# Graph layers with segment means and an edge softmax on one core: softmax weights in the bank of the logits, and the first mean pass scanning from PSUM

## The reference, cut to what matters

```python
# one SAGE layer; relu behind the first two
msg = x[src]
mean = segment_sum(msg, dst) / maximum(count(dst), 1)
h = mean @ Wl.T + bl + x @ Wr.T
# after three layers
x = layernorm(x + h)

# attention over the edges of each source node
q = (x @ Wq)[src];  k = (x @ Wk)[dst];  ek = edges @ Wek
v = (x @ Wv)[dst];  ev = edges @ Wev
attn = einsum('ehd,ehd->eh', q, (k + ek) * scale) @ W_exp
ex = exp(attn - segment_max(attn, src)[src])
attn = ex / segment_sum(ex, src)[src]
agg = segment_sum(attn * (v + ev), src)
out = ((x @ Wv) - agg) @ W_out
x = layernorm(x + out)
```

## Time and profile before

| What | us |
|---|---|
| median of three runs | 2773.49 |
| the runs | 2766.67 to 2774.2 |
| the profiled execution, its own time | 2783.83 |
| its span, first to last instruction | 2782.0 |
| POOL busy in the span | 1855.1 (67%) |
| PE busy in the span | 1887.0 (68%) |
| DVE busy in the span | 1732.6 (62%) |
| ACT busy in the span | 1098.7 (39%) |

### The profile page before, as it was taken

The page is one execution under the profiler, slowest core; times in us unless marked ns, Lnnn a source line. Parts: engine busy times, 40 slices in busy tenths (PEclk is TensorE's granted clock), DMA queues, the critical chain, the costliest instruction groups (busy, mean ns, idle before and its releaser), DMA issues.

```text
span 2782.0 us, 43790 instructions
## 1 busy us (share of the span) xinstructions
PE 1887.0 (68%) x10441; PEld 1352.4 (49%) x10441; DVE 1732.6 (62%) x5671; ACT 1098.7 (39%) x2508; POOL 1855.1 (67%) x1895
## 2 busy tenths in 40 slices
PE   3546666999979999677777745777777777770000
PEld 1425655666656666455555533555555555550000
DVE  7757777677757777565555533777777787780000
ACT  7951110444434444122222213666666666660000
POOL 0046776776647665377777777777777777745776
PEclk7657899999989999788888877999999999995555
DMA  0014654988869997544444513444444444433231
GB/s 18 1 50 126 148 142 115 184 198 187 188 139 172 192 203 165 146 126 130 123 136 136 155 42 100 133 136 134 136 139 134 138 136 140 133 110 106 85 96 54
DMA packets 366724, 356.94 MB, mean 128 GB/s; under 512 B 46534, under 2 KB 288724, under 8 KB 366584
## 3 DMA queue, kind: packets, MB, share of 16 engines
q1 hardware_dynamic: 310136, 246.40, 29.3%
q0 software_dynamic: 56448, 109.10, 20.6%
HBM read 232.83 MB, written 129.11 MB: 130 GB/s over the span
## 4 chain that ended last, share of the span: by engine, by line
POOL 36%; PE 28%; issue 18%; DVE 10%; DMA 5%; ACT 1%; SPq 1%; POOLq 1%; DVEq 0%; ACTq 0%
POOL hsrc L659 15%; POOL GX L659 14%; PE bank L836 7%; POOL out_dram L713 4%; PE bank L856 4%; PE bank L758 3%; PE bank L879 3%; PE bank L871 3%; PE bank L869 3%; DMA GX<-in_x_dram,idx_a 2%; POOL x_prime L713 2%; DVE hsrc L1200 2%; PE bank L840 2%; DVE hsrc L1201 1%; PE bank L854 1%
## 5 line engine op out<-in xcount | busy, mean ns | idle before, releaser
L659 POOL DMA_INDIRECT GX<-mean_product,idx_a x392 | 412.5, 1052 | 128.2 <-issue 114.4
L659 POOL DMA_INDIRECT GX<-in_x_dram,idx_a x392 | 406.2, 1036 | 118.3 <-issue 111.2
L1025 ACT ACTIVATE logv<-mv,eps 128x4 f32<-128x4 f32 x294 | 87.0, 296 | 586.6 <-DVE mv L1331 586.5
L836 PE MATMUL bank<-h,wt 128*128 128x512 f32 x588 | 316.1, 648 | 0.0
L1359 DVE TENSOR_TENSOR_SCAN seg<-flag,seg,hsrc 128x512 f32<-128x512 bf16 x147 | 189.2, 1287 | 147.4 <-ACT hsrc L1037 82.0
L713 POOL DMA_INDIRECT x_prime<-normed,idx_b x196 | 199.5, 1018 | 98.1 <-issue 92.1
L659 POOL DMA_INDIRECT hsrc<-x_prime,idx_d x196 | 216.5, 1105 | 59.8 <-issue 59.8
L758 PE MATMUL bank<-ident,GX 128*128 128x128 f32 x588 | 108.5, 315 | 214.1 <-DMA GX<-in_x_dram,idx_a 174.2
L659 POOL DMA_INDIRECT hsrc<-x_prime,idx_c x196 | 210.1, 1072 | 59.8 <-issue 59.8
L758 PE MATMUL bank<-ident,hsrc 128*128 128x128 f32 x468 | 92.4, 332 | 216.6 <-DMA hsrc<-x_prime,idx_d 123.2
L713 POOL DMA_INDIRECT out_dram<-XN,idx_b x196 | 192.5, 982 | 61.5 <-issue 53.3
(11 more groups left out here) (226 smaller groups left out, 4702.8 us busy)
## 6 DMA issues: line engine op xcount, KB each, us to landing
mean_product<-prod SPq DMA_DIRECT2D x147, 256.0 KB, 3.9
hsrc<-mean_product SPq DMA_DIRECT2D x147, 256.0 KB, 4.2
XN<-in_x_dram SPq DMA_DIRECT2D x98, 256.0 KB, 6.3
x_prime<-normed SPq DMA_DIRECT2D x98, 256.0 KB, 3.9
XN<-x_prime SPq DMA_DIRECT2D x98, 256.0 KB, 4.5
out_dram<-normed SPq DMA_DIRECT2D x98, 256.0 KB, 2.1
flag<-same_dst_row SPq DMA_DIRECT2D x147, 128.0 KB
XN<-low_row SPq DMA_DIRECT2D x98, 128.0 KB, 3.7
```

What stands on the lines that cost most here:

```text
L659: pool.indirect_dma_start(buf[:, c.slot(U), t, :], None, table, bass.IndirectOffsetOnAxis(ap=idx[:, c.slot(U), t:t + 1], axis=0)).then_inc ...
L836: last = pe.matmul(psum[:, :], wt[:, T_R[i], :], before[:, c.slot(2), :], start=True, stop=not dst_phase)
L1025: act.activation(logv[:, s, :], mv[:, s, :, 1], ACT.Ln, bias=eps[:, 0:1]).then_inc(n_log.of(c), 1)
```

## The change

1. `weight` is no longer a piece of SBUF but bank 5 itself. DVE writes logit - maximum back into bank 5, ACT takes the exponential of bank 5 in place, the den scan, the product with v and the num scan read it there, and the product writes it there. dmax keeps one half, for decay.
2. The logit matmul of a chunk, which overwrites bank 5, waits for the num scan of the chunk before (a_num) instead of its dmax.
3. In mean0 PE turns into bank 5 and bank 2 by turns. DVE scans from that bank and waits for the turn; ACT copies the bank to hsrc after the scan and waits for the scan. PE's turn waits for the scan and the copy of two chunks before, instead of the copy of one before.
4. The second pair of look-up banks of mean0 is 6 and 7 instead of 2 and 6, and one matmul of table_sums writes the upper half of bank 0 instead of bank 2.

mean1, mean2, dst and rest keep their code. On each engine the instructions stand in the same order as before; what differs is their operands and waits.

```diff
-        dmax = part([2, CH])
+        dmax = part([CH])
         decay = part([CH])
-        weight = part([CH])
+        weight = bank[5]
...
+        def turn_bank(c):
+            return (5, 2)[c.slot(2)]
...
             def mean_turn(c):
                 pe.wait_ge(gathered.of(c), gathered.after(c))
-                pe.wait_ge(m_h.of(c), m_h.after(c, 1))
-                psum = bank[5]
+                if c.phase == "mean0":
+                    pe.wait_ge(m_h.of(c), m_h.after(c, 2))
+                    pe.wait_ge(m_seg.of(c), m_seg.after(c, 2))
+                    psum = bank[turn_bank(c)]
+                else:
+                    pe.wait_ge(m_h.of(c), m_h.after(c, 1))
+                    psum = bank[5]
...
-                pe.matmul(bank[2][:, 0:COLS + 1], last_row[:, :], marks_sum[:, 1, :], start=True, stop=True).then_inc(marks_turned, 1)
+                pe.matmul(bank[0][:, WIDE:WIDE + COLS + 1], last_row[:, :], marks_sum[:, 1, :], start=True, stop=True).then_inc(marks_turned, 1)
...
-                return ((0, 1), (2, 6))[c.slot(2)] if c.phase == "mean0" else (3, 4)
+                return ((0, 1), (6, 7))[c.slot(2)] if c.phase == "mean0" else (3, 4)
...
             def att_logit(c):
                 pe.wait_ge(a_qk.of(c), a_qk.after(c))
-                pe.wait_ge(a_dmax.of(c), a_dmax.free(c))
+                pe.wait_ge(a_num.of(c), a_num.after(c, 1))
...
             def mean_keep(c):
-                act.wait_ge(m_turned.of(c), m_turned.after(c))
                 i = int(c.phase[-1])
+                if i == 0:
+                    act.wait_ge(m_seg.of(c), m_seg.after(c))
+                else:
+                    act.wait_ge(m_turned.of(c), m_turned.after(c))
                 h = take_cols(hsrc, c.index() * CH, CH)
                 if i == 0:
-                    act.activation(h, bank[5][:, :], ACT.Copy).then_inc(m_h.of(c), 1)
+                    act.activation(h, bank[turn_bank(c)][:, :], ACT.Copy).then_inc(m_h.of(c), 1)
...
-                act.activation(decay[:, :], dmax[:, 0, :], ACT.Exp)
-                act.activation(weight[:, :], dmax[:, 1, :], ACT.Exp).then_inc(a_exp.of(c), 1)
+                act.activation(decay[:, :], dmax[:, :], ACT.Exp)
+                act.activation(weight[:, :], weight[:, :], ACT.Exp).then_inc(a_exp.of(c), 1)
...
             def mean_seg(c):
-                dve.wait_ge(m_h.of(c), m_h.after(c))
+                if c.phase == "mean0":
+                    dve.wait_ge(m_turned.of(c), m_turned.after(c))
+                    rows = bank[turn_bank(c)][:, :]
+                else:
+                    dve.wait_ge(m_h.of(c), m_h.after(c))
+                    rows = take_cols(hsrc, c.index() * CH, CH)
...
-                dve.tensor_tensor_scan(seg[:, c.slot(2), :], flag[:, c.slot(4), :], take_cols(hsrc, c.index() * CH, CH),
+                dve.tensor_tensor_scan(seg[:, c.slot(2), :], flag[:, c.slot(4), :], rows,
...
-                dve.tensor_tensor(dmax[:, 0, :], prev, reset, ALU.add).then_inc(a_step1.of(c), 1)
-                dve.tensor_tensor(dmax[:, 1, :], logit, top, ALU.subtract)
+                dve.tensor_tensor(dmax[:, :], prev, reset, ALU.add).then_inc(a_step1.of(c), 1)
+                dve.tensor_tensor(weight[:, :], logit, top, ALU.subtract)
                 dve.wait_ge(a_step1.of(c), a_step1.after(c))
-                dve.tensor_tensor(dmax[:, 0, :], dmax[:, 0, :], top, ALU.subtract).then_inc(a_dmax.of(c), 1)
+                dve.tensor_tensor(dmax[:, :], dmax[:, :], top, ALU.subtract).then_inc(a_dmax.of(c), 1)
```

More of the change, by code:

```diff
@@ L1376, in make_table @@
                 dve.wait_ge(marks_turned, 1)
-                link(dve.tensor_copy(marks_r[:, :], bank[2][:, 0:COLS + 1]))
+                link(dve.tensor_copy(marks_r[:, :], bank[0][:, WIDE:WIDE + COLS + 1]))
                 for a in range(2):
@@ L1407, in look_take @@
                 s = c.slot(2)
-                banks, width, high = ((((0, 1), (2, 6))[s], COLS, high_src[:, :]) if c.phase == "mean0"
+                banks, width, high = ((((0, 1), (6, 7))[s], COLS, high_src[:, :]) if c.phase == "mean0"
                                       else ((3, 4), WIDE, col_f[:, 0, :]))
```

## The result

The changed kernel takes **2704.5 us** (median of five runs, 2701.5 to 2706.4), the kernel before 2773.7 (median of five, 2766.7 to 2778.1): a ratio of 0.975, with an interval from 0.973 to 0.976, or 69 us less. Its profiled execution took 2704.47 us (span 2702.6), as much as its median; that of the kernel before lies 10 us above its median, so the spans differ by 79 us.

What follows compares the result with a forecast made beforehand. GpSimd's indirect calls, stretched by VectorE instructions with two SBUF tensors, were taken as the bound. 23 (mean pass) + 1.5 (ahead of its loop) + 46 (attention) = 70.5 us off the median 2773.5 gave 2703 us, range 2683 to 2733.

Steps and rivals of the forecast that it cites:

- The bound and the mechanism: Mean pass and attention stage: GpSimd's indirect calls set the time; VectorE instructions reading two SBUF tensors hold them.
- The control L1452: Attention stage's maximum scan, data in bank 5, only flags from SBUF: all 48 calls beginning under it are unhindered.
- (2772 us): Rival: moving operands frees no calls; only the 1.5 us ahead of the mean pass's loop is gained; chance 0.03.
- Mean pass, 23 us: First mean pass's loop: scanning from PSUM removes 24.0 us of call stretch but 1 us; range 18 to 24.
- Two banks ahead of the loop, 1.5 us (0 to 2.5): Ahead of the mean pass's loop: scan no longer follows ScalarE's copy, 0.63 us a chunk, so the loop starts earlier.
- Attention stage, 46 us (24 to 62): Attention stage's calls: 61.7 us of stretch falls to 16 once L1465, L1468 and L1471 stop reading weight from SBUF.
- the random place of the beat: Attention stage: L1455, L1458, L1479 each hit 42% of chunks by 0.26 us on average, leaving 16 us in 49 chunks.
- The rival with every chunk hit, 38 us: Attention stage: remaining two-tensor instructions hold calls in every chunk, leaving 38 us instead of 16; 2725 us, chance 0.15.
- the cover of 1.8 us: Attention stage: gap between GpSimd's new period, about 15.5 us a chunk, and the other engines' floor of 13.7.
- Operands in PSUM, 0 (up to 10 us): Attention stage: reading and writing weight in bank 5 costs nothing; doubled in-place instructions would take 10 us of the gain.
- The slower rival (2808 us): Attention stage: four VectorE instructions on bank 5 take twice as long, 17.6 us a chunk, 59 us lost; chance 0.02.
- The new wait, 0: Attention stage: the logit matmul's wait for the previous chunk's num scan costs zero, since its att_qk wait ends later.

Runs made afterwards that it cites:

- each half alone: The kernel before with only the attention stage's part of the diff: 2730.5 us; with only the mean pass's part: 2755.0 us.
- the num scan put back: The changed kernel with the product weight * v written to SBUF, so the num scan reads two SBUF tensors again: 2718.1 us.
- decay in weight's stead: The changed kernel with decay kept in bank 5 and weight in SBUF: 2707.3 us.
- the bank alone: The kernel before with only mean0's second turn bank and moved look-up banks, its scan still reading hsrc behind the copy: 2777.0 us.

## Why the prediction was right, and where its terms were off

**The bound and the mechanism** held. The stages last as long as GpSimd's calls, and a VectorE instruction that reads two SBUF tensors holds the call that begins under it. This is shown from four sides: the whole change, each half alone, the num scan put back, and decay in weight's stead. The control L1452 had told it rightly: by the trace 60 calls begin under it, and none is held. The number of SBUF tensors isn't the whole rule, though. L1403 reads one (bf16) and a column of single numbers, and five calls that begin under it in the mean pass's loop end up to 0.13 us late; as it is short, they cost 0.5 us together.

**The rule of the Trainium skill.** "SBUF — State Buffer", Who interferes with whom, is borne out where it says that a VectorE instruction with two SBUF inputs contends with a GpSimd instruction that reads SBUF (42 calls of 48 held by the num scan with two, none by the den scan with one). The prediction read the inference that tensor_tensor leaves descriptor generation alone as if no such instruction held an indirect call (2772 us). That is not so: L1496 is a tensor_tensor and held 26. But the inference itself isn't refuted by it. These calls read their row numbers from SBUF, and they are held only near their start (see the last section), so it can be the reading that waits; no run separates it from the making of descriptors.

**Mean pass, 23 us.** The term that was mis-sized: 24.0 us of stretch came from a single execution, which lay at the top of a spread from 17 to 24. The half alone gave 19 us (interval 11 to 23). The rest left for L1403, 1 us, came out at nearly nothing. What is late next at the end of the pass had no term in the sum. In the two executions compared above the last call ends 27.5 us earlier and the last look-up is taken up only 24.5 us earlier, since it follows that call by 28.6 us and not by 25.6. But it follows it by 28.6 to 28.9 us in three of the four other executions that leave the scan alone, too (25.5 in the fourth), so these 3 us are no price of the change. The chain of waits in the loop (241 to 433 us) varies in the same way from one execution to the next; here are the two of the changed kernel, against the earlier trace rows:

```profile
by line: POOL GX L663 34.3%; issue 22.2%; PE bank L917 14.3%; PE bank L888 9.1%; DMA GX<-in_x_dram,idx_a 7.6%; DVE XN L1420 4.9%; PE bank L762 1.5%; DVE prod L1383 1.4%; DVEq L1429 1.4%; DVEq L1383 0.7%; DVE XN L1429 0.7%; POOL idx_a L653 0
```

```profile
by line: POOL GX L663 56.4%; issue 27.4%; DMA GX<-in_x_dram,idx_a 8.4%; PE bank L917 2.7%; PE bank L762 2.3%; PE bank L888 1.1%; POOL idx_a L653 0.8%; POOLq L679 0.3%; POOLq L463 0.3%; POOLq L139 0.2%; POOLq L678 0.1%; POOLq L653 0.1%; POOL
```

GpSimd and issue make 57% of the first and 84% of the second, as they did before; PE's look-ups (L917) and products (L888) make 23% and 4%. The last call ends at 432.3 and 433.6 us all the same. So PE comes close to the path in this loop, but no run shows that it costs time.

**Two banks ahead of the loop, 1.5 us (0 to 2.5).** The scan of the first chunk starts at 209.03 for 210.38, the index copies at 215.54 for 217.34, the loop 2.2 us earlier. Of this 0.6 us lie ahead of PE's first turn (207.93 for 208.55), where nothing changed. Counted from that turn the loop begins after 35.3 to 35.7 us in four executions with neither bank nor scan moved, and after 34.1 to 34.9 in seven with both: 1.1 us in the mean. With the bank alone it is 34.7. Inside the loop the banks brought nothing, as was said.

```profile
209.03 2.70 DVE L1376 TENSOR_TENSOR_SCAN seg<-flag,seg,bank 128x512 f32<-128x512 bf16 x2 [22.73 <-PE bank L762]
...
215.54 0.20 POOL L653 COPY idx_a<-col_i 128x16 int32 x1 [22.31 <-PE bank L762]
```

**Attention stage, 46 us (24 to 62).** By the calls it was 61.7 - 11.0 = 50.7, by the clock of the stage 51.2; the half alone shows 44 in the medians (interval 38 to 49). The step that was off is the random place of the beat, which gave each of three instructions some 5 us, 16 together. L1496 held 6.8 us, L1472 3.7 and L1475 none, together 10.5. Their places are not random, because one hold decides where the next call begins. L1475 begins 1.21 us behind L1472, nearly the 1.25 us from call to call: each of the 13 calls held under L1472 puts the next one 0.6 us into L1475, too late to be held, and a call that begins with L1472 is followed by one that begins with L1475. In a second execution of the changed kernel L1475 held two; with decay in the bank, where the distance is 1.33 us, it held 31. The num scan had shielded agg in the same way in the kernel before: the 43 calls held under L1471 put the next one 0.5 us into L1479, and of 47 calls there none was held. Why L1496 and L1472 are hit as often as they are stays open. The rival with every chunk hit, 38 us, falls. Its premise, that 46 of 49 calls begin under L1455, was misread too: 27 begin behind its start, of which 20 are held, and 20 more begin up to 0.2 us ahead of it.

**What comes next in the stage.** Forecast a period of 15.5 us, measured 15.39. GpSimd waits for PE 1.2 us in all, so the cover of 1.8 us over the others' floor sufficed.

**Operands in PSUM, 0 (up to 10 us).** Zero: 8 and 5 ns more on L1473 and L1485, less on the scans and the exponential than before. The slower rival (2808 us) falls with these rows.

**The new wait, 0.** PE's waits in the attention stage name only att_qk (L1457) ahead of the logit matmul, at most 0.5 us a time (0.7 for its weight load), much as in the kernel before (16.1 us, 37 times); the num scan before it doesn't appear:

```profile
PE bank L971 <- DVE hsrc L1457: 18.8, 43, 0.5
```

**The sum.** 2703 forecast, 2704.5 measured, is closer than its terms, and that is luck: the mean pass was some 4 us too large, the attention stage some 5 too small by the calls, and the two cancel. Taken off the profiled execution the same sum gave 2713, where 2704.5 was measured. What stays open is why the profiled executions of the kernel before (2779 to 2784 us) lie above its medians (2774 to 2778) while those of the changed kernel do not; its times vary from 2767 to 2791 us over the chips, and stretch measured in the profiled ones may be a few us larger than in a median run.

## What to carry to other kernels

Where GpSimd's indirect calls set the pace, count the SBUF tensors that VectorE's instructions read beside them: a second operand that is in PSUM already, or can stay there, cost VectorE nothing here and took 69 us off 2774. Look for a control in the trace first, an instruction of the same length with another mix of operands. And take the size of a stretch, and the shares of a chain, from more than one execution: the mean pass's stretch lay between 17 and 24 us with no change of code.

## What was not expected of the hardware

**A hold sets the beat.** The end of a held call fixes where the next ones begin, so that two scans with two SBUF tensors each cost 50 us together, and one of them alone 17. Stretches of this kind don't add up.

**A call that comes first wins.** In the kernel with the product in SBUF a call that began at 2111.03 took 0.94 us, though L1473 with two SBUF tensors started at 2111.16, inside it:

```profile
2111.03 0.94 POOL L664 DMA_INDIRECT hsrc<-x_prime,idx_d  x1 [0.30 <-issue]
2111.16 0.69 DVE L1473 TENSOR_TENSOR hsrc<-hsrc,flag 128x512 f32<-128x512 f32 x1
```

So the call wasn't held, nor did the VectorE instruction take longer than its usual 0.69. This is the rule and no single case: 45 calls of that kernel's attention stage were under way when the num scan, with two SBUF tensors, began; none of them took more than 947 ns, and the scan no more than its 1.28 us. In the changed kernel nine calls that began 0.035 to 0.044 us behind the start of L1472 weren't held either; there L1472 took 0.76 to 0.77 us for its usual 0.69. Those that began later, up to 0.49 us behind its start, were all held. So what makes a call wait lies near its start, and the rest of it, some 0.75 us, runs unhindered beside a VectorE instruction with two SBUF tensors.

**ScalarE is a little faster in PSUM.** The exponential of 128x512 takes 579 ns from bank to bank and took 614 from SBUF to SBUF. Whether the input's place or the output's does it wasn't tested; a copy of that size from a bank to SBUF (L1093) takes 579 as well.
